# Linear attention and MLP block: attention loop written out, zero matmuls at the start, raw weight copies later, prologue norm and last chunk reordered

## What is computed

```
def _L0_attn_ref(x, ...):                      # x is xn
    h = rmsnorm(x, attn_norm_w)
    x = x + linear_attention(h, Wq, Wk, Wv, Wo, out_norm_w)
    h = rmsnorm(x, mlp_norm_w)
    return x + silu(h @ Wgate) * (h @ Wup) @ Wdown

def step(S, (qb, kb, vb)):                     # per head, chunk by chunk
    attn = where(causal, qb @ kb.T, 0.0)
    o = attn @ vb + qb @ S
    return S + kb.T @ vb, o                    # o is then rmsnormed and projected by Wo

xn = _layernorm(x)
s = _L0_attn_ref(xn, ...)
g = silu(fp4_linear(silu(fp4_linear(xn, w_gate)) * fp4_linear(xn, w_up), w_down))
return x + s * g
```

## Time and profile before

| | us |
|---|---|
| median of 3 runs | 1136.68 (1136.5 to 1137.47) |
| profiled execution | 1137.76 |
| its span | 1136.0 |
| mean granted clock of PE | 0.994 of full |
| PE busy / DVE busy / ACT busy / POOL busy | 1098.6 / 892.5 / 510.4 / 53.3 |

### The profile page before, as it was taken

How to read it: one execution, slowest core, us unless ns; L and a number is a source line. 1 busy time by engine, 2 the same in 40 slices (tenths; PEclk the granted TensorE clock), 3 DMA queues, 4 the chain that set the end, 5 groups by cost and what they waited for, 6 DMA issues and landing times.

```text
span 1136.0 us, 21922 instructions
## 1 busy us (share of the span) xinstructions
PE 1098.6 (97%) x7124; PEld 1004.8 (88%) x7124; DVE 892.5 (79%) x1948; ACT 510.4 (45%) x1414; POOL 53.3 (5%) x74
## 2 busy tenths in 40 slices
PE   5999999999999999999999799999999999999998
PEld 4888998888998889998998699999999999999997
DVE  5688888788888888888667877777877778778787
ACT  5554644546545456465453533333433333333332
POOL 1000000000000000000000101001020202020200
PEclk9999999999999999999999899999999999999999
DMA  8444444544444445444436300111111102011010
GB/s 279 140 162 139 156 132 146 161 140 135 162 141 145 143 139 175 139 136 136 143 121 210 121 19 20 55 37 55 37 55 37 55 19 74 19 51 41 19 56 19
DMA packets 99095, 118.38 MB, mean 104 GB/s; under 512 B 7824, under 2 KB 90640, under 8 KB 98960
## 3 DMA queue, kind: packets, MB, share of 16 engines
q1 hardware_dynamic: 98912, 115.16, 31.1%
q0 software_dynamic: 96, 2.16, 0.5%
HBM read 68.98 MB, written 50.48 MB: 105 GB/s over the span
## 4 chain that ended last, share of the span: by engine, by line
PE 77%; DVE 12%; DMA 4%; issue 4%; ACT 2%; SPq 1%; DVEq 0%
PE ps L221 60%; PE ps L626 4%; PE ps L585 3%; PE ps L620 3%; PE ps L606 3%; DMA moved<-work 2%; PE ps L713 2%; DMA r_gate<-moved 2%; PE ps L657 1%; DVE work L1181 1%; DVE work L1225 1%; DVE work L1199 1%; DVE work L1185 1%; ACT onT L845 1%; DVE work L1149 1%
## 5 line engine op out<-in xcount | busy, mean ns | idle before, releaser
L221 PE MATMUL ps<-r_k,r_gate_up 128*128 128x512 f32 x768 | 188.7, 396 | 4.3 <-DVE work L1342 4.3
L221 PEld LDWEIGHTS ps<-r_k,r_gate_up 128*128 128x128 f32 x768 | 141.8, 189 | 32.5 <-DVE work L1342 4.8
L855 ACT ACTIVATE work<-ps 128x128 f32<-128x128 f32 x256 | 67.5, 279 | 98.3 <-PE ps L626 98.3
L221 PE MATMUL ps<-r_o,onT 128*128 128x256 f32 x768 | 107.0, 288 | 0.1
L221 PE MATMUL ps<-hT,r_k 128*128 128x512 f32 x384 | 106.1, 412 | 0.9 <-DVE hT L1088 0.9
L221 PEld LDWEIGHTS ps<-r_q,r_v 128*128 128x128 f32 x768 | 100.6, 193 | 5.9 <-issue 2.0
L221 PE MATMUL ps<-r_q,r_v 128*128 128x256 f32 x768 | 104.3, 286 | 0.0
L972 ACT ACTIVATE r_v<-work 128x512 fp32r<-128x512 f32 x64 | 40.5, 632 | 131.6 <-DVE work L1342 131.6
L221 PE MATMUL ps<-hT,r_q 128*128 128x512 f32 x384 | 99.2, 394 | 0.0
L221 PE MATMUL ps<-r_v,hT 128*128 128x512 f32 x384 | 97.4, 390 | 0.0
L221 PEld LDWEIGHTS ps<-r_o,onT 128*128 128x128 f32 x768 | 95.7, 190 | 0.3 <-DVE onT L1100 0.3
(11 more groups left out here) (145 smaller groups left out, 2058.7 us busy)
## 6 DMA issues: line engine op xcount, KB each, us to landing
moved<-work SPq DMA_DIRECT2D x63, 512.0 KB, 2.9
r_gate<-moved SPq DMA_DIRECT2D x252, 128.0 KB, 2.5
work<-kept SPq DMA_DIRECT2D x17, 514.0 KB, 5.3
work<-in_L_attn_hidden_states SPq DMA_DIRECT2D x16, 512.0 KB, 4.6
kept<-work SPq DMA_DIRECT2D x9, 514.0 KB, 3.9
work<-kept_xq SPq DMA_DIRECT2D x9, 512.0 KB, 3.2
kept_xq<-work SPq DMA_DIRECT2D x8, 512.0 KB, 3.1
out<-work SPq DMA_DIRECT2D x7, 512.0 KB, 3.5
```

The costliest lines, as they stand in the source:

```text
L221: done = pe.matmul(out_ap, a, b, start=first and n == 0, stop=last and n == 2, skip_group_check=skip)
L855: done = act.activation(squares[:, c, :], ps[:, B_O, c * P:(c + 1) * P], ACT.Square, accum_out=small[:, OS, c:c + 1])
```

## The change

- **Loop**: the three-pass loops over batches on PE, VectorE, ScalarE and SP become Python loops, so the code stands three times and no register or jump is left. The loops over blocks in `networks` stay.
- **Zero matmuls**: PE runs six f32 matmuls of 512 columns on a cleared tile (`leaving`, plane 1) into bank B_O, before anything else.
- **Raw weight copies**: POOL's three transfers into `raw4` now stand behind its two memsets and wait for k_tok_ready of 2. SP's wait for them moves from ahead of its loop into step 3 of batch 0, ahead of the first load from `raw4`.
- **Prologue norm**: VectorE computes the RMS factor before `normalize`, and counts each normalized chunk (`first_xn`). ScalarE's h copies follow chunk by chunk and stand ahead of weight_hi(2), and VectorE's weight_lo(2) stands behind `turned_lo`.
- **Last chunk**: `last_down4` does the products with hqT's high part first, then those with the low part, in bank B_GATE. VectorE does `hq_lo` ahead of the residual addition in the last block.

```diff
@@ SP @@
                     if h == 3 and not final:
+                        if n == 0:
+                            sp.wait_ge(raw4_gathered, 48)
                         sp.wait_ge(piece_stored, 16 * n + 16)
...
-                sp.wait_ge(raw4_gathered, 48)
-                with sp.Fori(0, batches - 1) as b:
+                for b in range(batches - 1):
@@ POOL @@
-                pool.wait_ge(w_loaded[len(w_parts) - 1], 16)
+                pool.wait_ge(w_ready, len(w_parts))
+                pool.memset(attn, 0.0).then_inc(attn_cleared, 1)
+                pool.wait_ge(attn_cleared, 1)
+                pool.memset(x2, 0.0).then_inc(x2_summed, 1)
+                pool.wait_ge(k_tok_ready, LAG)
                 for i, w in enumerate((w_gate, w_up, w_down)):
                     pool.dma_start(raw4[i * NET4:(i + 1) * NET4].rearrange("(a b) -> a b", b=w.shape[1]), w)\
                         .then_inc(raw4_gathered, 16)
                 pool.sem_inc(piece_stored, 16)
-                pool.wait_ge(w_ready, len(w_parts))
-                pool.memset(attn, 0.0).then_inc(attn_cleared, 1)
-                pool.wait_ge(attn_cleared, 1)
-                pool.memset(x2, 0.0).then_inc(x2_summed, 1)
@@ PE @@
+                pe.wait_ge(leaving_clear, 1)
+                for i in range(WARM):
+                    pe.matmul(ps[:, B_O, :], leaving[:, 0, 1, :], leaving[:, :, 1, :], start=True, stop=True)
                 pe.wait_ge(s_const, 5)
                 pe.wait_ge(h_ready, 1)
                 turn_h(0)
...
-                with pe.Fori(0, batches - 1) as b:
+                for b in range(batches - 1):
...
+                def last_down4(n, c):
+                    for f in range(T4):
+                        if f in (0, FIRST4):
+                            pe.wait_ge(hq_hi, (n * CH + c) * 2 + (1 if f == 0 else 2))
+                        parts = (HI, LO) if f < FULL4 else (HI,)
+                        for a in parts:
+                            pe.matmul(ps[:, B_GATE, 0:D], hqT[:, HI, f, :], wdown4[:, a, f, :],
+                                      start=f == 0 and a == HI, stop=False)
+                    for f in range(T4):
+                        if f in (0, FIRST4):
+                            pe.wait_ge(hqT_ready, (n * CH + c) * 2 + (1 if f == 0 else 2))
+                        done = pe.matmul(ps[:, B_GATE, 0:D], hqT[:, LO, f, :], wdown4[:, HI if f < FULL4 else LO, f, :],
+                                         start=False, stop=f == T4 - 1)
+                    done.then_inc(out4_done, 1)
@@ ACT @@
                 ln_sqrt(2)
+                for c in range(CH):
+                    if c < CH - 1:
+                        act.wait_ge(first_xn, c + 1)
+                    else:
+                        act.wait_ge(xn_ready, 1)
+                    done = act.activation(h_sb[:, c, :], xn[:, 0, c, :], ACT.Copy, scale=small[:, HR, c:c + 1])
+                done.then_inc(h_ready, 1)
                 weight_hi(2)
                 act.wait_ge(s_nw, 48)
-                normed_h(0, 1)
                 turned_hi(0, 0, 1)
...
-                with act.Fori(0, batches - 1) as b:
+                for b in range(batches - 1):
@@ DVE @@
                 ln_second(0, 1, before)
-                normalize(0)
-                rms_factor(2, 1, before)
+                dve.wait_ge(ln_root_ready, 2)
+                inverse_root(LNA, LNR, small[:, HR, :], before)
+                normalize(0, first_xn)
                 weight_lo(0)
                 weight_lo(1)
-                weight_lo(2)
                 dve.wait_ge(s_nw, 48)
                 turned_lo(0, 0, 1)
                 turned_lo(1, 0, 2)
+                weight_lo(2)
...
-                with dve.Fori(0, batches - 1) as b:
+                for b in range(batches - 1):
...
+                    if final:
+                        hq_lo(n, CH - 1)
                     dve.wait_ge(mlp_done, n + 1)
...
                     dve.tensor_tensor(res, ps[:, B_MLP:B_MLP + 2, :].rearrange("p a (c d) -> p (a c) d", d=D),
                                       x2b[:, :, 0:D], ALU.add).then_inc(sum_read, 1)
-                    hq_lo(n, CH - 1)
                     if not final:
+                        hq_lo(n, CH - 1)
```

More of the change, by code:

```diff
@@ L232, in build @@
         PLAIN = STEPS - LAG - 1
+        WARM = 6
         FIRST_V_BANKS = (B_O, B_STATE, B_TURN, B_Y)
@@ L244, in build @@
         xq_ready, xq_stored = sem("xq_ready"), sem("xq_stored")
-        x_loaded, xn_ready = sem("x_loaded"), sem("xn_ready")
+        x_loaded, xn_ready, first_xn = sem("x_loaded"), sem("xn_ready"), sem("first_xn_chunks")
         ln_arg_ready, ln_root_ready, rr_ready = sem("ln_arg_ready"), sem("ln_root_ready"), sem("rms_factor_ready")
@@ L798, in networks @@
                         gate_up4(n + 1, 0)
-                    down4(n, CH - 1)
+                        down4(n, CH - 1)
+                    else:
+                        last_down4(n, CH - 1)
                 with pe.Fori(0, BLOCKS - 1) as n:
@@ L809, in normed_h @@
                 def normed_h(parity, value):
-                    act.wait_ge(rr_ready, value)
+                    act.wait_ge(rr_ready, value - 1)
                     for c in range(CH):
@@ L979, in hq, with gate_out @@
                            .then_inc(hq_hi, 1)
-                def gate_out(n, c):
+                def gate_out(n, c, bank=B_OUT4):
                     act.wait_ge(out4_done, n * CH + c + 1)
-                    act.activation(g4[:, c, :], ps[:, B_OUT4, 0:D], ACT.Silu).then_inc(g4_ready, 1)
+                    act.activation(g4[:, c, :], ps[:, bank, 0:D], ACT.Silu).then_inc(g4_ready, 1)
                 def weights4_hi(i, k):
@@ L1030, in networks @@
                         silu4(n + 1, 0)
-                    gate_out(n, CH - 1)
+                    gate_out(n, CH - 1, B_GATE if final else B_OUT4)
                 with act.Fori(0, BLOCKS - 1) as n:
@@ L1071, in ln_second, with normalize @@
                     dve.tensor_scalar(small[:, LNA, :], u, EPS, None, ALU.add).then_inc(ln_arg_ready, 1)
-                def normalize(parity):
+                def normalize(parity, chunk_done=None):
                     for c in range(CH):
@@ L1077, in normalize @@
                                                  rstd[:, parity, c:c + 1], ALU.subtract, ALU.mult)
+                        if chunk_done is not None and c < CH - 1:
+                            done.then_inc(chunk_done, 1)
                     done.then_inc(xn_ready, 1)
```

## The result

| | before | after |
|---|---|---|
| median | 1136.64 (6 runs, 1135.64 to 1138.64) | 1131.92 (6 runs, 1130.25 to 1132.29) |
| ratio to before, 95% interval | | 0.9953 (0.9940 to 0.9965) |
| profiled execution / span | 1137.76 / 1136.0 | 1130.51 / 1128.8 |

The forecast was 1127.3 with a range of 1123.5 to 1130.8. The sign was right, the size was not: 4.7 us by the medians, 7.2 by the spans, against 9.4. The executions of one kernel differ by 2 to 3 us.

What follows compares the result with a forecast made beforehand. PE, busy for 97% of the span, was taken to bound the kernel. The terms -6.6 - 1.0 - 4.4 + 1.9 + 0.7 gave -9.4, so 1127.3 us against the median of 1136.68; range 1123.5 to 1130.8.

Steps and rivals of the forecast that it cites:

- Part 1: Batch loop written out: the steps ending passes 1 and 2 fall to 9.77 us; -6.6 us, bounds -5.5 and -7.
- the rule: About 108 ns per compare-and-branch: the loop's two jumps cost an estimated 0.2 us, and the sum would be -3.0.
- D: The loop's stall belongs to that place of the code and returns when written out: +6.4, 1133.7 us; chance 0.04.
- E: Written-out code is fetched late and VectorE stalls 2.5 us at five places in two passes: 1139.8 us; chance 0.03.
- A: Prologue: clock stays high from the zero matmuls through the k projection, 1.3 us less, 1126.0 us; chance 0.17.
- B: Early steps: the third exchange's loads slip through between the raw copies, 1125.4 us; chance 0.14.
- Part 2: Prologue norm and zero matmuls: first k projection starts at 14.2, first scores at 25.1; -1.0 us.
- The other end: Prologue: the most the zero matmuls could bring, a k projection at the high clock, -1.3 us; gain 0 was taken.
- Part 3: Raw weight copies moved later: the first exchange's store lands sooner, -4.4 us; the third exchange is held, +1.9 us.
- The term of +1.9: Step 2: the third exchange's loads, partly held by raw copies, land 13.6 after scores(1); bounds 0 and +3.2 us.
- rival C: Raw copies hold the third exchange to their end, PE's wait brings the low clock: 1.3 + 1.6 more, 1130.2; chance 0.14.
- Part 4: Last chunk: the hq split goes first and the residual sum ends later; +0.7 us, between 0 and +0.9.

Runs made afterwards that it cites:

- e6: The kernel before with the batch loop written out on PE, ScalarE and SP and kept on VectorE alone: 1136.77 us, ratio 0.9995 to before.
- e7: The kernel before with the batch loop written out on VectorE, ScalarE and SP and kept on PE alone: 1128.50 us, ratio 0.9919 to before.
- e4: The changed kernel without the six matmuls of zeros: 1131.89 us, ratio 0.9950 to before.
- e9: The changed kernel without raw copies, residual addition first in the last block, nine zero matmuls instead of six: 1122.11 us, ratio 0.9868 to before.
- e5: The changed kernel without raw copies and with the residual addition ahead of the hq split in the last block: 1124.47 us, ratio 0.9886 to before.
- e8: The changed kernel with raw copies written into padded rows, so packets are of 2.8 KB: 1132.87 us, ratio 0.9961 to before.
- e1: The kernel before with only the batch loop written out, on PE, VectorE, ScalarE and SP: 1126.88 us, ratio 0.9910 to before.
- e12: The kernel before with the batch loop written out on VectorE alone: 1129.16 us, ratio 0.9931 to before.

## Why the prediction failed, step by step

**Part 1, loop: right in mechanism, its size 2.9 too small.** The two steps came to 9.78 and 9.78, as forecast from the third pass. What was missing is a second term, put at nothing without a reason: I compared looped steps with looped steps and took the jump for the loop's only cost. The rows of before could have told: VectorE's idle time ahead of L1278 was 0.24 to 0.62 us in each looped step and 0.17 or 0.18 in the steps of the last batch that were written out. The lengths of the steps tell less, since step 53, the written-out like of step 5, took 9.77 against 9.86.

**The other rivals and the rule.** D and E did not come: in after VectorE has no idle time of 2.5 us at the ends of the passes, and no step within them is over 10 us. Nor did A, since the k projection took 2.90 us, nor B, since the loads were held. The jump cost 2.5 us on VectorE where it was on the path (e6: 2.59 idle), and nothing visible on PE (e7). The 108 ns that the Trainium skill (Advanced Engine Details and Errata, Control Flow Timing) gives for a compare and branch did not describe a jump of VectorE's here; the rows of before had said so.

**Part 2.** The projection started 9.6 after the statistics began, against 10.75: -1.15, forecast -1.0. In the profiled execution x landed 0.65 later, which hid half of it: the scores came at 25.57 and not at 25.1. The size was partly luck: some 0.45 of the 1.15 is the clock at the transposes (9.6 after the statistics in after, 10.04 in e4), which I had not counted, and the reordering gave the rest. In the time the zero matmuls were worth nothing that shows (0.9953 with, 0.9950 without). The other end, 1.3 us for a k projection at the high clock, was right (e9: 1.64 us instead of 2.90).

**Part 3, the step that failed.** Up to the scores of step 1 the forecast held: 33.12, forecast 32.6, with the store of 2.9 us. Then "the store's neighbours can slip between them, so I take 13.6": the loads landed so that VectorE began at 49.58, 16.5 after scores(1), beyond even my bound of 14.9. The term of +1.9 measured +6.6, and the start as a whole +1.9 where the forecast was -3.5 and its worst bound -1 (which the text does not work out; its own bound of +3.2 gives -2.2). Two things were wrong. I took the store's 10.1 us in before as the longest hold, though 367 of its packets had gone through in 2.1 us on the way and its own transfer was part of the 10.1; loads that are shut out to the end begin their own 3 us only then, and from the copies' issue to VectorE's start it was 11.2 us. Another 0.5 is that POOL issued the copies later than I had taken. And I priced the low clock in rival C only, at 1.6, while it lasted 6.8 us and cost 2.1: the step was 6.6 longer, and PE's wait was 4.5 of it. Rival C was the right mechanism, too small and with too small a chance.

**Part 4: right.** +0.7, measured +0.68, for the reason given, and e5 shows the converse.

**The range.** By the step sums, -9.4 should have been -6.6 - 2.9 for the loop, -4.8 for the start up to the scores of step 2, +6.6 for step 2 and +0.5 for the rest: -7.2, as the spans have it. Two errors stood against each other: without the loop's 2.9 the gain would have been 4.3 by the spans. With 7.2 off its median the kernel would have been within the range, and that would have been luck. The remaining 2.5 to the medians is between executions: before's profile was above its median, which I had taken into account, after's was below, which cannot be seen ahead. Why after's median lies above its profile is not settled. The mean clock does not tell: the two executions at 0.990 took 1132.04 and 1132.29, but of the three at 0.992 one took 1130.25 and another 1132.25, and only one execution was profiled.

## What to carry to other kernels

Before a large transfer is moved off one wait, look at what it will stand in front of at its new place, price it as its full length plus the held transfer's own, and add the low clock that PE's wait brings; better still, ask whether it is needed, since a loop that is written out may make a staging buffer useless. Write out or keep the loop engine by engine: only the engine that the others wait for pays. Work that is put ahead of a wait on another engine only helps if it is not itself waiting, and work that could fill that wait belongs in front of it.

## What the runs showed of the hardware

- A transfer of POOL's software queue shut SP's queue out almost wholly: 16 packets in 5.5 us, with packets of 22 to 45 KB (after), and none in 4 us with packets of 2.8 KB (e8), after which the two queues shared. In before, 173 got through in the 1.0 us in which no large packet of the copies began, and 194 in the next 1.1 us beside them. What decides this was not tried.
- The jump back of a loop left VectorE idle for 2.5 us, PE's was hidden (e6, e7). In the loop VectorE stood idle 0.07 us more ahead of L1278 in each step, and 0.43 more in three of them (before, e6; not in e1 and e12).
- Matmuls of zeros brought PE to the high clock: the ninth took 1.02 us in e9. With PE idle for 1.72 and 0.52 us around the transposes the k projection took 1.64 us (e9). With 2.22 and 1.37 the granted clock was 0.50 from 14.4 on and it took 2.90 (after). With 3.40 ahead of them the transposes were slow as well, 1.94 us (e5).
